# Two-layer transformer kernel: another order of work in the layer-norm stage of the first layer

## The reference, cut to what matters

```python
def _layernorm(x, axis=-1, eps=1e-05):
    m = jnp.mean(x, axis=axis, keepdims=True)
    v = jnp.var(x, axis=axis, keepdims=True)
    return (x - m) / jnp.sqrt(v + eps)
...
    # layer 0, on the normalised x
    qk = (x @ Wqk_w.T + Wqk_b).reshape(b, n, H, E, 2)
    v = (x @ Wv_w.T + Wv_b).reshape(b, n, H, E)
    scores = jnp.einsum('bhqd,bhkd->bhqk', q, k)
    attn = jax.nn.softmax(scores, axis=-1) / ...
    ...
    logits = x_flat @ W_router.T
    probs = jax.nn.softmax(logits, axis=-1)
    topk_probs, topk_idx = jax.lax.top_k(probs, TOP_K)
    h = jnp.einsum('nd,erd->ner', x_flat, A)
    base_out = x_flat @ W_base.T + b_base
```

## Time and profile before

| | us |
|---|---|
| median of three runs | 1468.0 |
| lowest and highest of them | 1464.19, 1468.36 |
| the profiled execution | 1465.94 |
| its span in the trace | 1464.0 |

### The profile page before, as it was taken

How to read it: one execution, slowest core, us unless ns; L and a number is a source line. 1 busy time by engine, 2 the same in 40 slices (tenths; PEclk the granted TensorE clock), 3 DMA queues, 4 the chain that set the end, 5 groups by cost and what they waited for, 6 DMA issues and landing times.

```text
span 1464.0 us, 21333 instructions
## 1 busy us (share of the span) xinstructions
PE 1373.5 (94%) x7350; PEld 1076.4 (74%) x7350; DVE 981.1 (67%) x1834; ACT 855.6 (58%) x2103; POOL 634.2 (43%) x973
## 2 busy tenths in 40 slices
PE   4989988899999999999999999999999999989997
PEld 3733336688888788877888887888778877768786
DVE  6665655577777776777777777777687777675333
ACT  2345564566667666676666666676666666563211
POOL 4322365544355544444444554544444545433311
PEclk9998998899999999999999999999999999999999
DMA  4200031101020110012011101101020111114010
GB/s 141 65 1 1 1 97 58 44 1 59 4 71 21 39 53 22 30 30 74 1 60 35 40 24 36 60 15 40 21 73 4 42 35 38 37 58 135 15 58 29
DMA packets 35882, 61.01 MB, mean 42 GB/s; under 512 B 9056, under 2 KB 13280, under 8 KB 35776
## 3 DMA queue, kind: packets, MB, share of 16 engines
q1 hardware_dynamic: 35776, 59.66, 12.9%
HBM read 49.68 MB, written 9.96 MB: 41 GB/s over the span
## 4 chain that ended last, share of the span: by engine, by line
PE 75%; DVE 12%; issue 7%; ACT 3%; POOL 2%; DMA 1%; POOLq 0%; DVEq 0%; SPq 0%; ACTq 0%
PE T L2298 7%; PE T L1910 7%; PE T L1912 6%; PE T L1911 6%; PE S L1912 5%; PE S L1911 5%; PE S L1910 5%; PE WB L1910 4%; PE VB L1912 4%; PE VB L1910 4%; PE WB L1911 4%; PE WB L1912 4%; PE VB L1911 4%; PE VB L2066 2%; PE T L2181 2%
## 5 line engine op out<-in xcount | busy, mean ns | idle before, releaser
L881 POOL TENSOR_TENSOR RI<-SM,C 128x1 f32<-128x1 f32 x256 | 142.9, 558 | 506.8 <-ACT PB L1214 505.7
L1682 DVE CUSTOM_DVE_ANT_0 PB<-S,REL,SLC 128x128 f32<-128x128 f32 (+7 forms) x256 | 204.5, 813 | 80.3 <-PE S L1912 78.7
L1214 ACT ACTIVATE PB<-PB,NM 128x128 f32<-128x128 f32 (+7 forms) x256 | 198.9, 777 | 69.2 <-DVE NM L1682 64.3
L1287 ACT ACTIVATE R<-T 128x512 fp32r<-128x512 f32 x288 | 170.5, 593 | 100.6 <-PE T L2298 98.6
L1689 DVE TENSOR_TENSOR R<-T,R 128x512 fp32r<-128x512 f32 x288 | 197.5, 689 | 42.1 <-ACT R L1287 23.7
L882 POOL TENSOR_SCALAR PB<-PB,RI 128x128 f32<-128x128 f32 (+7 forms) x256 | 214.5, 838 | 25.2
L2298 PE MATMUL T<-C,PB 128*128 128x128 f32 x1152 | 176.6, 276 | 11.9 <-DVE R L1689 6.7
L2298 PEld LDWEIGHTS T<-C,PB 128*128 128x128 f32 x1152 | 134.2, 140 | 48.0 <-DVE R L1689 18.0
L1194 ACT ACTIVATE JUNK<-WB 128x128 bf16<-128x128 f32 x252 | 66.2, 277 | 93.1 <-PE WB L1912 93.1
L1910 PE MATMUL T<-R 128*128 128x512 f32 x256 | 104.0, 406 | 3.9 <-issue 2.1
L1912 PE MATMUL T<-R 128*128 128x512 f32 x256 | 100.5, 393 | 0.0
(11 more groups left out here) (299 smaller groups left out, 3521.1 us busy)
## 6 DMA issues: line engine op xcount, KB each, us to landing
RAW<-w SPq DMA_DIRECT2D x86, 256.0 KB, 2.8
DQ<-codes SPq DMA_DIRECT2D x16, 352.0 KB, 3.5
DQ<-absmax SPq DMA_DIRECT2D x16, 352.0 KB, 2.9
dequantised<-DQ SPq DMA_DIRECT2D x16, 352.0 KB, 2.2
PB<-x SPq DMA_DIRECT2D x12, 256.0 KB, 3.3
PB<-dequantised SPq DMA_DIRECT2D x5, 512.0 KB, 4.5
PB<-x_scratch SPq DMA_DIRECT2D x8, 256.0 KB, 3.9
out<-PB SPq DMA_DIRECT2D x8, 256.0 KB, 2.0
```

The source lines that it names most:

```text
L881: ch.link(e.tensor_tensor(RI[:, k:k + 1], SM[:, k:k + 1], C[:, C_EXP + 5:C_EXP + 6], ALU.pow))
L1214: e.activation(pb(m, a, 0, L), pb(m, a, 0, L), ACT.Exp, scale=-1.0, bias=NM[:, k:k + 1], accum_out=SM[:, k:k + 1]).then_inc(exp_done, 1)
L1287: e.activation(r(PT + AT[i, ("PV", kb)] % 3 * 1024, 512), T[AT[known, it] % 2][:, :], ACT.Copy).then_inc(t_act, 1)
L1682: e.tensor_tensor_reduce(out=pb(m, a, 0, L), in0=bank[:, 0:L], in1=REL[:, TOK - L:TOK], scale=SLC[:, a:a + 1], scalar=3.0e38, op0=ALU.add, ...
```

## The change

The change rewrites the stage up to M7 and leaves what is behind it.

1. **Lists.** Tables `LN_PE`, `LN_ACT`, `LN_DVE` and `LN_POOL` give the order up to Q2 on each engine. On PE the V products of tiles 0 to 4 stand among the transposes, one tile behind, and X7 stands behind Q0.
2. **Apply on ACT.** DVE only computes minus mean times reciprocal root (N(t), 128x1), and ACT makes the normalised tile as an activation with scale and bias (A(t), `apply0`).
3. **Banks.** The V products leave the ring and take the banks VB and WB in turn, with semaphores of their own.
4. **Chunks.** The V weights come first: W0 and W1, then the query and key weights as W2 to W4. W2 to W4 have places of their own (in G, which is not in use yet), as have tiles 4 to 7. SP asks for all of these without a wait. W5 and W6 wait for `split` at 2, W7 to W9 as before.
5. **Behind Q2.** PE: M0, V5, V6, M1, V7, Q3, M2, Q4, M3, M4, Q5, M5, Q6, M6, Q7, M7. ACT: V5, W5, V6, W6, V7, W7, W8, W9, the bias row, the exponential, Q3. The constant for the output bias (`ones_set`) is now ACT's first instruction. DVE computes the masks behind S1, and joins Q3 ahead of reduction 6; the comparisons of the router stand behind reduction 8.

```diff
-L0_CHUNKS = (_cut(0, WQK_H, WQK_L, 2048, RAWC) + _cut(2048, WVAR_H, WVAR_L, KT * NVAR, 512)
+L0_CHUNKS = (_cut(2048, WVAR_H, WVAR_L, KT * NVAR, 512) + _cut(0, WQK_H, WQK_L, 2048, RAWC)
...
-W0_QK, W0_VAR, W0_BASE, W0_EXP, W0_O = 3, 5, 8, 9, 10
+W0_VAR, W0_QK, W0_BASE, W0_EXP, W0_O = 2, 5, 8, 9, 10
...
+LN_PE = ("X0", "X1", "X2", "V0", "X3", "V1", "X4", "V2", "X5", "V3", "X6", "V4", "Q0", "X7", "Q1", "Q2")
...
+X0 = XS + [G[:, t * D:(t + 1) * D] for t in range(4)]
+W0_STAGE = [G[:, 2048:2816], G[:, 2816:3584], G[:, 3584:4096]]
...
-                if q >= 2:
-                    sp.wait_ge(split, q - 1)
+                sp.wait_ge(split, 2 if q < 7 else q - 1)
...
+            first_chunk(0)
+            first_chunk(1)
+            sp.dma_start(ROWS[:, 0:R_BO], rows[:, 0:R_BO]).then_inc(in_bv, 16)
+            late_x(4)
+            late_x(5)
+            first_chunk(2)
+            late_x(6)
+            late_x(7)
+            first_chunk(3)
+            first_chunk(4)
+            sp.dma_start(ROWS[:, R_BO:NROWS], rows[:, R_BO:NROWS]).then_inc(in_rows, 16)
             for q in range(5, NL0):
                 src, _, _, n = L0_CHUNKS[q]
                 raw(q, w0[:, src:src + n])
...
+            def apply0(t):
+
+                act.wait_ge(nb_ready, t + 1)
+                if t >= 4:
+                    act.wait_ge(t_full, T_A["X", t - 4] + 1)
+                e.activation(XN[t % 4], X0[t], ACT.Identity, bias=NB[:, t:t + 1], scale=RSTD[:, t:t + 1]).then_inc(xn_ready, 1)
...
+                elif what == "N":
+                    dve.wait_ge(var_ready, t + 1)
+                    dve.wait_ge(rstd_ready, t + 1)
+                    e.scalar_tensor_tensor(NB[:, t:t + 1], MV[:, t, 0:1], -1.0, RSTD[:, t:t + 1], ALU.mult, ALU.mult)\
+                        .then_inc(nb_ready, 1)
...
-                k = T_A["VAR", t]
-                ring(k)
+                pe.wait_ge(split, W0_VAR)
+                pe.wait_ge(t_free, T_A["X", t] + 1)
+                if t >= 2:
+                    pe.wait_ge(var_free, t - 1)
...
+            max0(0)
+            var(5)
+            var(6)
+            max0(1)
+            var(7)
+            qk(*QK_THEN[0])
+            max0(2)
+            qk(*QK_THEN[1])
             max0(3)
-            qk(*QK_THEN[0])
             max0(4)
-            qk(*QK_THEN[1])
+            qk(*QK_THEN[2])
```

More of the change, by code:

```diff
@@ L906, in _ @@
             hold(pool, pad_set, 1, p_passed)
[L907 to L917, removed]
+            for what, q in LN_POOL:
+                q = int(q)
+                if what == "R":
+                    rstd(q)
+                else:
+                    _, hi, lo, n = L0_CHUNKS[q]
+                    low_half(q, hi, lo, n)
             tri = C[:, C_TRI:C_TRI + 64].unsqueeze(1).to_broadcast([P, NT, 64])
@@ L1097, in qk @@
                 qk_halves(i, blk, T[k % 2])
[L1099 to L1102, removed]
-                k = T_A["VAR", t]
[L1104 to L1107, removed]
+            e.activation(r(PT + 2560, P, 64), IDENT[0:64, :], ACT.Copy, scale=0.0, bias=1.0 / 32).then_inc(ones_set, 1)
+            for what, t in LN_ACT:
+                t = int(t)
+                if what == "W":
+                    high_half(t, L0_CHUNKS[t][1], L0_CHUNKS[t][3])
+                elif what == "A":
+                    apply0(t)
+                elif what == "X":
+                    high_xt(T_A["X", t], t)
+                elif what == "V":
+                    high_var(t)
+                else:
+                    if t == 0:
+                        act.wait_ge(masks_ready, 5)
+                    qk(t, *QK_FIRST[t])
             act.wait_ge(in_rows, 16)
             e.activation(r(PT + 2048, D, 64), ROWS[0:64, R_BO:R_BO + D], ACT.Copy).then_inc(bo_high, 1)
-            e.activation(r(PT + 2560, P, 64), IDENT[0:64, :], ACT.Copy, scale=0.0, bias=1.0 / 32).then_inc(ones_set, 1)
             act.wait_ge(row_ready, 1)
@@ new lines, in _ @@
+            for what, t in LN_DVE:
+                t = int(t)
+                if what == "S":
+                    dve.wait_ge(in_x[t] if t < 4 else in_late[t - 4], 16)
+                    stats(t, X0[t])
+                elif what == "N":
[3 more added lines that the diff above has]
+                        .then_inc(nb_ready, 1)
+                elif what == "X":
+                    low_xt(T_A["X", t], t)
+                elif what == "V":
+                    if t == 0:
+                        dve.wait_ge(in_bv, 16)
+                        dve.wait_ge(vf_clear, 2)
+                    var(t)
+                else:
+                    qk(t, *QK_FIRST[t])
+                if what == "S" and t == 1:
+                    set_masks()
@@ L1484, in _ @@
+            max0(0)
[4 more added lines that the diff above has]
+            var(7)
+            max0(3)
             ch.settle()
             ch.done(e.tensor_reduce(RT[:, 3, 0:NT], by_e(0), AX.X, ALU.max))
+            max0(4)
+            ch.settle()
+            e.tensor_tensor(by_e(1), by_e(0), over_e(RT[:, 3, 0:NT]), ALU.subtract).then_inc(row_ready, 1)
+            max0(5)
+            qk(3, *QK_THEN[0])
+            dve.wait_ge(row_exp, 1)
+            ch.done(e.tensor_reduce(RT[:, 3, 8:16], by_e(2), AX.X, ALU.add))
@@ L1934, in _ @@
             pe.wait_ge(in_const, 16)
-            for t in range(NT):
-                transpose_x(T_LN0 + t, t, t + 1)
             def qk(blk, nt):
```

206 lines of the change are left out of this document (98 added, 108 removed).

## The result

The changed kernel takes 1472.97 us in the median (11 runs, 1471.10 to 1480.17), the kernel before on the same chip 1467.73 (11 runs, 1463.48 to 1469.68). The ratio is 1.0047 with a 95% interval of 1.0032 to 1.0062. By the medians it is 5.2 us slower; the ratio is worked out from all runs and makes it 6.9 us. The profiled execution took 1477.43 us, with a span of 1475.3. It is 4.5 us above the median, and I come back to why.

The account below looks back on a forecast made before the run. PE was taken as bound by waits at the start, then PE and DVE together from 43.6 us. Front, M0 to M4 and M4 to TS gave 78.1, clock 2.3: TS 80.4, +3.7 on 1465.94, 1469.6 us, rounded 1470; range 1463 to 1476.

Parts of the forecast that it names:

- the slower rival: Clock also low in Q products Q0 and Q1: M0 at 44.3 to 46.3, upper part 1473.8 us; chance 0.28.
- The sum: Profiled 1465.94 us plus the stage-end shift of 3.7 us: 1469.6 us, rounded to 1470.
- TS: Time of the transposes on line 2024 ending the stage's written-out order; forecast to move from 76.7 to 80.4 us.
- hole ahead of M4: PE idle from 55.3 to 61.2 us, 5.9 us, waiting for reductions 6 and 7 behind Q3's join.
- Masks, table load, loads without waits: Start of the stage: table load gains 1.3 us on ACT; X0 starts at 9.3 us as before; landing stops being a bound.
- The small bias: DVE's NB in the tile loop, replacing DVE's apply, was put at 0.1 us per tile.
- the walk: Engine lists stepped through in order with row durations and 0.05 us per hand-over; half a microsecond off on the old order.
- Chunks, then Q3: Copies of W5 to W9 on ACT hold Q3's halves until 56.5 us; M0 to M4 takes 19.2 us against 16.2.
- The clock ahead of TS: Holes on PE before M4, M0, X5, X6 and Q1 lower the clock: 0 to 6.4 us, taken as 2.3.
- Behind TS: Same work in the same order, so only the shift of TS counts; low clock stretches give plus or minus 3 us.
- Faster only with an M0 at 38: Rival: Q3's halves don't wait, M4 at about 57.5, 1463.6 us, needing M0 at 38 instead of 42; chance 0.10.

Follow-up runs that it names:

- a1_again: The changed kernel run and profiled once more, unaltered; 1474.7 us against 1466.5 for the kernel before.
- b2: Kernel before with only the output-bias constant made ACT's first instruction, so the table load comes early; 1465.7 us against 1467.5.
- e5: Changed kernel with the apply taken back to DVE, at the place of N(t); 1471.2 us against 1467.3 for the kernel before.
- e6: Changed kernel with the apply left on ACT and the small bias made by POOL; 1476.1 us against 1467.3 for the kernel before.
- e1: Changed kernel with Q3's halves and the exponential ahead of W8 and W9 on ACT; 1472.8 us against 1466.5 for the kernel before.
- e2: Changed kernel with ACT's copies of W5 to W9 ahead of and between Q0 to Q2 and V5 to V7; 1471.7 us against 1466.5 before.
- e3: Changed kernel with 20 unused matmuls added on PE between M3 and M4; 1471.4 us against 1466.5 for the kernel before.
- e4: Changed kernel with unused matmuls added: 9 ahead of M0, 14 between M3 and M4, 9 ahead of TS; 1467.6 us against 1467.3 before.
- e7: Kernel of e2 with Q7 behind M7, as before the change; 1471.4 us against 1467.3 for the kernel before.
- h2: Changed kernel with e2's early copies, PE's own products spread into the holes and DVE's joins behind a pair's second reduction; 1464.9 us against 1467.5 before.
- h3: Kernel of h2 with the apply on DVE as in e5; 1462.26 us against 1468.15 for the kernel before, ratio 0.9976.
- b1: Kernel before with only Q7 moved ahead of M7 on PE; 1469.2 us against 1467.5.
- after: The changed kernel itself, first measurement and profile; 1472.97 us against 1467.73 for the kernel before.

## Why the prediction was right

The time was forecast at 1470 in a range of 1463 to 1476, and is 1473.0. The shift of 5.2 us is 0.36%, just beyond the 0.3% that the prediction took as telling. The mechanism was the forecast's. The size lies between the forecast and the slower rival (1473.8), and nearer to the rival, whose mechanism, a low clock in the Q products, the first profile does not show. The sum gave 1469.6, 3.4 us too low: 1.8 since it starts from the profiled execution (1465.94) and not from the median (1467.7), 1.1 at TS, and 0.4 beyond TS. Point by point, in us:

| step | forecast | measured |
|---|---|---|
| X0, X3, X4, X6 | 9.3, 16.2, 19.7, 26.8 | 9.4, 16.9, 21.0, 28.2 |
| Q0, Q1, M0 | 28.7, 34.0, 42.0 | 30.1, 35.4, 43.3 |
| W5's and W9's copies | 44.6, 55.2 | 46.5, 57.3 |
| Q3's halves, reduction 6, M4 | 56.5, 58.7, 61.2 | 58.5, 60.7, 63.1 |
| hole ahead of M4 | 5.9 | 4.6 (5.3 in a1_again) |
| M0 to M4 | 19.2 | 19.8 |
| M4 to TS | 16.9 and the clock | 18.4 |
| TS | 80.4 | 81.5 |

- **Masks, table load, loads without waits**: X0 came where it should. That the load gives nothing at X0 was right. Its worth in the old order (2.1 us at M0, by b2) was not seen in the prediction, and so neither that the change loses it elsewhere.
- **The small bias** is the term that was mis-sized. "DVE's NB costs 0.1" was 1.19 us in two of the eight tiles. X4 was 1.3 us later than the walk, and 1.3 to 1.4 us stay in every later row up to M0. From M0 to TS the walk with its clock was 38.4 us, and the trace has 38.2. e5 and e6 price it at 1.5 to 1.7 us from X0 to X6. I had counted POOL's disturbance against the 128x512 apply alone. The Trainium skill, SBUF — State Buffer, section SBUF: two separate sides, has the rule that I missed: a VectorE operation with two inputs in SBUF and a GpSimd operation that reads SBUF exclude each other for the whole instruction. The trace agrees, with 1.19 us until POOL's 1.83 us are over and 0.31 until its 1.26 are; N(0) with its 0.10 is the row against it.
- **Chunks, then Q3**: right in every link. W5 to W9 took 10.8 us (forecast 10.6), and e1 shows that they held M4. It was not the only wait, as e2 shows with the exponential.
- **The clock ahead of TS**: of "0 to 6.4, I take 2.3", e3 shows 1.8 in M4 and Q5 and e4 another 1.3 between M0 and M3, some 3 together. That the slower rival depends on the length of the holes, 1.94 us being the mark, was too simple. Holes of 2.03 and 2.04 us ahead of X6 left it high in five executions and were followed by the low level in three (a1, e7, h2). In just these three all of X3 had still been at the low level (1.09 us; 0.63 to 0.92 in the five), so how late the clock had risen goes with it there. e6 fits (X3 1.05, low), e5 (0.79, low) and h3 (1.06, high) do not.
- **Behind TS** I had written the shift of TS and plus or minus 3 us. The hole of 2.08 us ahead of TS, from Q7's new place, was not in the prediction. In the table, the seven kernels with a hole of 2.1 us there have lost 0.1 to 4.7 us beyond TS, 2.4 in the mean, and the five with none above 0.8 have -1.6 to +0.4. b1, with 2.88 us and -0.9, speaks against it. That a drop of the clock follows the hole is seen in all eight, within 7 us, while the five without (and before) have the full clock for 12 us or more behind TS. Its cost is not shown. TS is from one execution of each, so a single entry is good to 2 us or so. In the profiles the attention took 149.2 us in three of the seven, but 138.2 to 141.7 in the other four (before 140.6), and 145.8 and 146.9 in h2 and h3, which have no such hole.
- **Faster only with an M0 at 38**: this was wrong. e2 has the copies early with M0 at 43.3, by another place in ACT's list; what would make it faster was the order of PE's own products, which I had not asked about.

## What to carry to other kernels

When work is moved out of a stretch, ask what it covered there: the three V products (V2 to V4) that moved ahead of M0 had been what kept PE busy between the pairs, and they left holes which cost first the wait and then the clock. Put real work into each wait in the order, one piece per wait, and split a piece in two where a wait is shorter than it. A small instruction is only cheap alone: price it by what runs beside it, and test each part of a change by itself: the early table load alone was worth 2.1 us at M0, and the parts around it hid that.

## What the runs showed of the hardware

- A DVE operation on 128x1 with two SBUF operands took 1.19 us across a POOL subtraction of 1.83 us and ended with it (14.68 to 15.87 beside 14.03 to 15.86), against 0.14 to 0.18 alone. The same operation for tile 1 took 0.31, 0.79 and 0.97 us in after, a1_again and e2, and each time ended within 0.02 us of POOL's subtraction.
- The clock behind a hole of about 2 us is not settled by the order. The hole ahead of X6 was 2.03 us in after (clock high) and in a1_again (low), 1.84 in e5 (low) and 1.85 in h3 (high). From X6 to M0 it was 15.1 to 15.2 us in the six profiles with the clock high and 16.7 in the five with it low: 1.5 us lost.
- In the attention of the first layer the low time was 6.8 to 36.3 us over fourteen profiles of the same work, and the stretch took 137.2 to 149.2 us, in the main longer with more low time (13.6 us of it in 140.6 before, 20.1 in 141.7 in a1_again, 35.9 in 149.2 in after). The 3 to 15 us by which runs of one kernel spread may come from there; that was not measured run by run.
- The table load, issued at 0.72 us before any input had landed, took the same 1.28 us and delayed nothing.
